# Second combination, normalisation and router products moved into the second attention's block of a two-layer transformer kernel

## The reference, cut to what matters

```python
xn = _layernorm(x)
x = x + _L0_attn_ref(xn, ...) + _L0_ffn_ref(xn, ...)
xn = _layernorm(x)
x = x + _L1_attn_ref(xn, slope_rate, Wqkv, Wg, norm_w, Wo) + _L1_ffn_ref(xn, router_w, ...)

# _L1_attn_ref: 16 heads of 128, linear attention with a decay per head
qkv = silu(x @ Wqkv.T)                 # q, k, v of every head
out = scan over blocks: (q * q_decay) @ kv + ((q @ k.T) * diag_decay) @ v
out = out * rsqrt(mean(out * out) + eps) * norm_w
return (sigmoid(x @ Wg.T) * out) @ Wo.T

# _L1_ffn_ref: one of 8 experts per token
router_logits = x @ router_w.T         # the best logit chooses the expert, its sigmoid scales the row
```

## Time and profile before

| what | value |
|---|---|
| median of 3 runs | 1422.84 us (1420.04 to 1425.09) |
| profiled execution, its own time | 1426.64 us |
| its span in the profile | 1424.8 us |
| PE busy (matmul) | 1279.2 us, 90% |
| DVE, ACT, POOL busy | 658.3, 526.1, 702.4 us |
| first transfer of combine1 issued at | 418.39 us |
| first product of attention1 at | 485.15 us |
| attention1's head loop | 492.6 us to about 1186 us |

### The profile page before, as it was taken

One profiled execution on the slowest core, in us unless ns is written; L12 is line 12 of the kernel. 1 busy time (PEld: TensorE's weight loads), 2 busy tenths in 40 slices (PEclk: granted clock), 3 DMA queues, 4 the chain that ended last, 5 costly groups with the idle time before them and its releaser, 6 DMA issues. The chain is left out here.

```text
span 1424.8 us, 20402 instructions
## 1 busy us (share of the span) xinstructions
PE 1279.2 (90%) x7238; PEld 1039.0 (73%) x7267; DVE 658.3 (46%) x1346; ACT 526.1 (37%) x1122; POOL 702.4 (49%) x556
## 2 busy tenths in 40 slices
PE   4488799999955388999999999999999996999999
PEld 4366588788845377888888888888888883666655
DVE  4698555565426247654554443534343341222223
ACT  2344466565535322333433334333343331111110
POOL 3343466676633646666776654756555540000014
PEclk9999999999985699999999999999999997999999
DMA  6700277777745321122212112111111106511113
GB/s 219 267 1 1 62 155 157 149 155 154 166 109 172 109 63 34 53 66 69 75 45 67 48 60 64 49 60 34 60 49 34 45 0 244 202 45 45 45 59 115
DMA packets 98483, 128.43 MB, mean 90 GB/s; under 512 B 11728, under 2 KB 81232, under 8 KB 98256
## 3 DMA queue, kind: packets, MB, share of 16 engines
q1 hardware_dynamic: 83408, 100.90, 22.2%
q0 software_dynamic: 14976, 26.23, 9.6%
HBM read 98.88 MB, written 28.21 MB: 89 GB/s over the span
## 5 line engine op out<-in xcount | busy, mean ns | idle before, releaser
L1553 PE MATMUL a_p_p<-a_xr,a_wr 128*128 128x512 f32 x1152 | 307.9, 403 | 2.4 <-DVE g_x L1957 2.4
L1553 PEld LDWEIGHTS a_p_p<-a_xr,a_wr 128*128 128x128 f32 x1152 | 207.7, 189 | 41.2 <-DVE g_x L1957 3.1
L1786 POOL TENSOR_TENSOR a_sqsum<-a_sqsum,a_sq 128x512 f32<-128x512 f32 x60 | 77.7, 1296 | 221.9 <-ACT a_sq L1710 221.9
L365 POOL DMA_INDIRECT acc<-l_ye,g_slot_token x64 | 102.1, 1595 | 67.1 <-ACT l_ye L695 57.7
L1565 PE MATMUL a_p_p<-a_wvr,a_xr 128*128 128x512 f32 x384 | 105.8, 413 | 24.1 <-POOL a_wvr L1755 24.1
L1751 POOL TENSOR_TENSOR a_wr<-a_w,a_wr 128x768 fp32r<-128x768 f32 x64 | 124.2, 1942 | 1.7 <-DVE a_wr L1812 1.7
L1844 DVE SCALAR_TENSOR_TENSOR a_gated<-a_th,a_p_o 128x512 f32<-128x512 f32 x64 | 44.0, 688 | 159.9 <-ACT a_sq L1710 159.9
L1788 POOL TENSOR_TENSOR a_gr<-a_gated,a_gr 128x512 fp32r<-128x512 f32 x64 | 97.6, 1525 | 23.7 <-DVE a_gr L1848 23.7
L1221 POOL DMA_DIRECT2D out<-e_ye x24 | 13.1, 546 | 193.5 <-DVE e_ye L1371 193.5
L1615 PE MATMUL a_p_w<-a_gr,l_wo_r 128*128 128x512 f32 x384 | 100.1, 396 | 2.3 <-POOL a_gr L1788 2.3
L1565 PEld LDWEIGHTS a_p_p<-a_wvr,a_xr 128*128 128x128 f32 x384 | 69.5, 194 | 36.4 <-issue 24.2
(11 more groups left out here) (248 smaller groups left out, 2761.8 us busy)
## 6 DMA issues: line engine op xcount, KB each, us to landing
a_w<-in_Wqkg SPq DMA_DIRECT2D x64, 384.0 KB, 3.2
l_up<-in_gate_up SPq DMA_DIRECT2D x64, 192.0 KB
a_wv<-in_Wv SPq DMA_DIRECT2D x16, 512.0 KB, 4.3
e_up<-in_gate_up SPq DMA_DIRECT2D x8, 1024.0 KB, 13.6
l_down<-in_down SPq DMA_DIRECT2D x64, 96.0 KB
acc<-l_zero SPq DMA_DIRECT2D x2, 2176.0 KB, 11.8
f_part<-acc SPq DMA_DIRECT2D x8, 512.0 KB, 6.2
e_down<-in_down SPq DMA_DIRECT2D x8, 512.0 KB, 12.3
```

Source lines behind the costliest of these rows:

```text
L365: pool.indirect_dma_start(g["acc"][e % 2][:, :], rows(e), ye[e % YR][:, :], None, compute_op=ALU.add)\
L1553: mm = pe.matmul(dst[:, :], wr[n % 2][:, wp, kk, c * P:(c + 1) * P], xr[n // H1 % 2][:, xp, kk, :], start=(kk, xp, wp) == (0, 0, 0), stop= ...
L1786: pool.tensor_tensor(sqsum[b % 2][:, :], sqsum[b % 2][:, :], sq[a % 2][:, :], ALU.add).then_inc(summed, 1)
```

## The change

`combine1` is gone, and its work stands in `attention1`, between the pieces of the prologue and in steps 0, 2, 5 and 8. The partial sums are loaded into tiles that the loop uses later (`qk` and `v[1]`), the raw output weights into `ywT`. The x of batches 0 and 1 is no longer read back from `cols1`, but split from `xT` as ACT leaves it there; `cols1` is still stored. A tile's logits share a PSUM bank with its transpose and are copied out tile by tile, where a copy of all stood at the end. The output weights are split in quarters: the first ahead of the loop, the others at n = 2, 5 and 8, by ACT in one operation for each head and by DVE (which takes the place of POOL). The pieces of the expert choice come later: `choose` at 2, the two rank products at the `state` of 3 and 4, `count` at 6, `place_experts` at 7, `place_rows` at 8, `tile_experts` at 9, `row` from 10 on.

```diff
-def combine1(nc, io, g):
...
+    CHOOSE, RANKS, ROWS = 2, (3, 4), 10
...
+        wo = ywT[:, :, :].rearrange("p k n -> p (k n)").rearrange("p (h n) -> p h n", h=QUAD)
+        part = [[qk[:, 2 * i:2 * i + 2, :].rearrange("p a n -> p (a n)").rearrange("p (t d) -> p t d", t=DB) for i in range(2)],
+                [v[1][:, 2 * i:2 * i + 2, :, :].rearrange("p t h e -> p (t h e)").rearrange("p (t d) -> p t d", t=DB) for i in range(2)]]
...
@@ sync @@
+            parts(0)
...
             values(0)
+            parts(1)
             weights(0)
+            output_weights(0)
             weights(1)
+            parts(2)
+            parts(3)
             values(1)
...
+            for c in range(DB):
+                store_columns(c)
             for n in range(LAST):
+                if n in (1, 4, 7):
+                    output_weights((n + 2) // 3)
                 if n + 2 < N:
                     weights(n + 2)
...
@@ tensor @@
+            def turn_x(t):
+                pe.wait_ge(xn_ready, t + 1)
+                if t >= 2:
+                    pe.wait_ge(logits_kept, t - 1)
+                for kk in range(KD):
+                    mm = pe.transpose(p_w[t % 2][:, kk * P:(kk + 1) * P], xn[t % 4][:, kk * P:(kk + 1) * P], g["ident"][:, :])
+                mm.then_inc(x_in_psum, 1)
+
+            def route_logits(t):
+                c, i = divmod(t, DB)
+                pe.wait_ge(xT_kept, t + 1)
+                for kk in range(KD):
+                    mm = pe.matmul(p_w[t % 2][:, 2 * P:2 * P + E1], xT[c % 2][:, kk, i * P:(i + 1) * P], router[:, kk, :],
+                                   start=kk == 0, stop=kk == KD - 1)
+                mm.then_inc(routed, 1)
+
+            def columns(c):
+                for t in range(DB * c, DB * (c + 1)):
+                    turn_x(t)
+                    if t % DB:
+                        route_logits(t - 1)
+                route_logits(DB * c + DB - 1)
...
-            for t in range(DB):
-                value(0, t)
+            pe.wait_ge(router_in, 16)
+            columns(0)
+            value(0, 0)
+            value(0, 1)
+            columns(1)
+            value(0, 2)
+            value(0, 3)
+            columns(2)
             for n in range(LAST):
                 a = n - 1
                 if n < N:
                     project(n, 0)
-                if n == 1:
-                    ranks()
                 if 0 <= a < N:
                     score(a)
                 if n < N:
                     project(n, 1)
+                if n == 0:
+                    columns(3)
...
@@ scalar @@
+            ins.then_inc(decays_done, 1)
+            root(0)
+            columns(0)
+            root(1)
+            high_output(0)
+            root(2)
+            value(0, 0)
+            value(0, 1)
+            columns(1)
+            root(3)
+            value(0, 2)
+            value(0, 3)
+            columns(2)
             for n in range(LAST):
...
+                if n == 0:
+                    columns(3)
+                if n in (2, 5, 8):
+                    high_output((n + 1) // 3)
...
@@ gpsimd @@
+            join(0)
+            low_v(0)
+            join(1)
+            low_w(0)
             low_x(0)
-            low_v(0)
-            low_w(0)
+            join(2)
+            pool.wait_ge(decays_done, 1)
+            pool.tensor_tensor(g["decay"][:, :, :], g["decay"][:, :, :], causal[:, :].unsqueeze(1).to_broadcast([P, H1, P]),
+                               ALU.mult).then_inc(causal_done, 1)
+            join(3)
             low_w(1)
+            low_x(1)
             low_v(1)
...
@@ vector @@
+            def low_output(i):
+                dve.wait_ge(wo_high, i + 1)
+                for h in range(QUAD):
+                    at = QUAD * i + h
+                    ins = dve.scalar_tensor_tensor(g["wo_r"][:, 1, at, :], wo[:, h, :], half_norm[:, at:at + 1], g["wo_r"][:, 0, at, :],
+                                                   ALU.mult, ALU.subtract)
+                ins.then_inc(wo_parts, 1)
...
+            combine(0)
+            high_v(0)
+            normalise(0)
+            combine(1)
+            high_w(0)
             high_x(0)
-            high_v(0)
-            high_w(0)
+            normalise(1)
+            combine(2)
             high_w(1)
+            normalise(2)
+            combine(3)
+            high_x(1)
+            normalise(3)
+            dve.wait_ge(half_ready, 1)
+            low_output(0)
             high_v(1)
             for n in range(LAST):
...
+                if n in (2, 5, 8):
+                    low_output((n + 1) // 3)
                 route(n)
...
-                spent = combine1(nc, io, g)
-                spent += attention1(nc, io, g)
+                spent = attention1(nc, io, g)
```

More of the change, by code:

```diff
@@ L1609, in output @@
                 if n == 0:
-                    pe.wait_ge(rank_kept, 2)
+                    pe.wait_ge(logits_kept, NT)
+                if h % QUAD == 0 and n < H1:
+                    pe.wait_ge(wo_parts, h // QUAD + 1)
                 if h == 0 and n:
@@ L1710, in square, with root, columns @@
                 act.activation(sq[n % 2][:, :], p_o[:, :], ACT.Square).then_inc(squared, 1)
-            for t in range(DB):
-                value(0, t)
+            def root(c):
+                act.wait_ge(var_ready, c + 1)
+                act.activation(std[:, DB * c:DB * (c + 1)], veps[:, DB * c:DB * (c + 1)], ACT.Sqrt).then_inc(std_ready, 1)
+            def columns(c):
+                if c >= 2:
+                    act.wait_ge(cols_stored[c % 2], 16)
+                    act.wait_ge(x_parts, c - 1)
+                for t in range(DB * c, DB * (c + 1)):
+                    i = t % DB
+                    act.wait_ge(x_in_psum, t + 1)
+                    act.activation(xT[c % 2][:, :, i * P:(i + 1) * P], p_w[t % 2][:, 0:2 * P].rearrange("p (k n) -> p k n", k=KD), ACT.Copy)\
+                        .then_inc(xT_kept, 1)
+                    if i:
+                        keep_logits(t - 1)
+                keep_logits(DB * c + DB - 1)
@@ new lines, in _ @@
+            act.wait_ge(c_in, 96)
+            act.activation(g["kdec"][:, :], slope[:, :], ACT.Exp, scale=back[:, :])
+            act.activation(g["bdec"][:, :], slope[:, :], ACT.Exp, scale=float(-P))
+            act.wait_ge(slope_ready, 1)
+            for h in range(H1):
+                act.activation(g["qdec"][:, h, :], ramp[:, :], ACT.Exp, scale=minus_slope[:, h:h + 1])
+            for h in range(H1):
+                ins = act.activation(g["decay"][:, h, :], lag[:, :], ACT.Exp, scale=minus_slope[:, h:h + 1])
@@ new lines, in normalise @@
+            def normalise(c):
+                at = slice(DB * c, DB * (c + 1))
+                dve.wait_ge(std_ready, c + 1)
+                dve.reciprocal(g["norm"][:, at, 1], std[:, at]).then_inc(rstd_ready, 1)
+                dve.wait_ge(rstd_ready, c + 1)
+                for t in range(DB * c, DB * (c + 1)):
+                    if t >= 4:
+                        dve.wait_ge(x_in_psum, t - 3)
+                    dve.tensor_scalar(xn[t % 4][:, :], g["x"][:, t, :], g["norm"][:, t, 0:1], g["norm"][:, t, 1:2],
+                                      ALU.subtract, ALU.mult).then_inc(xn_ready, 1)
```

320 lines of the change are left out of this document (118 added, 202 removed).

## The result

| what | before | after |
|---|---|---|
| median | 1422.78 us, 8 runs (1418.70 to 1425.09) | 1410.82 us, 8 runs (1408.61 to 1420.03) |
| profiled execution, its span | 1426.64, 1424.8 us | 1409.83, 1408.0 us |
| first transfer of the changed stretch | 418.39 | 413.11 |
| first product of step 2, counted from that transfer | 96.0 | 79.5 |
| first expert product, counted from that transfer | 777.0 | 764.4 |

The medians differ by 12.0 us. The ratio after to before is 0.9928 with the interval 0.9912 to 0.9944, which makes it 10.2 us faster, between 8.0 and 12.5. The forecast was 7.2 us faster (a median of 1415.6), so its sign and range were right and its size too small.

The account below looks back on a forecast made before the run. PE was taken as the bound, at 10.37 us a loop step. A gain of 8.0 us by step 2 and 0.8 lost in the loop made -7.2 us, so median 1422.84 becomes 1415.6; range 1404 to 1424.

Parts of the forecast that it names:

- Part 1: Prologue up to the first value product: it can start at 447.8, 37.4 us earlier than 485.15.
- The round of 1.8 us: Per-tile round of transpose, logits and their copy in the prologue's chunks: 1.8 us, bounds 1.2 and 2.3.
- The lock: DVE against POOL: with POOL work queued, DVE gets one SBUF operation through per POOL operation; normalise(1) then ends at 457.2.
- Rival B: DVE gets its four prologue normalisations in between POOL's operations; all behind is 7.1 earlier, 1408.5 us; chance 0.25.
- The table loads: Prologue switches from Sqrt to Silu on ACT: 1.28 us per load, next activation right behind, without the 1.38 drain.
- part 2: Prologue from first value to step 2: most of the 37.4 given back; step 2 at 506.4, 8.0 us gained.
- rows 2: Busy times per stretch before the change: PE at granted clock 0.50, 1.2 GHz, between 440 and 460 us.
- rival C: Clock stays at 2.4 GHz through columns(2) and (3): 4.1 us less, 1411.5 us; chance 0.10.
- The loop: Head loop: new DVE pieces stall steps by 7.9 us together, 0.8 more than the 7.06 removed.
- Rival D: DVE's backlog at steps 2, 5 and 8 stalls attend each time: 21.2 instead of 7.9, 1428.9 us; chance 0.15.
- Rival E: Prologue chunks wait for each other across ACT, DVE and POOL, eight microseconds more: 1423.6 us; chance 0.08.
- old stall: In attend of step 4 before the change: 4.72 us waiting for DVE's decay; removing it gives 7.06 us.

Follow-up runs that it names:

- mask_late: The kernel after with POOL's masking of the decays moved behind join(2), low_w(1), join(3) and low_x(1): 1409.51 us, ratio 0.9866 to the kernel before.
- columns_together: The kernel after with columns(2) directly behind columns(1), and value(0, 2) and value(0, 3) after both: 1416.24 us, one run, against 1422.62 for the kernel before.
- tiles_last: The kernel after with 13 small tiles declared behind the large ones: 1410.91 us, ratio 0.9918 to the kernel before.
- all_together: The kernel after with mask_late's POOL order, tiles_last's declarations and output-weight quarters at steps 1, 3 and 11: 1399.92 us, ratio 0.9827 to the kernel before.
- all_again: The kernel of all_together, unchanged, run once more for its trace: 1404.19 us, one run, against 1430.13 for the kernel before.
- second pair of profiles: Kernels before and after, unedited, profiled once more: before 1425.01 us (one run), after 1416.89 us, ratio 0.9924.
- ranks_only: The kernel before with only the two rank products moved, from ahead of score(0) to behind attend(0): 1421.53 us, ratio 0.9960.

## Why the forecast was right, and where it was not

**Part 1 held.** The first root was forecast at 437.1 and came at 437.4, the first value product at 447.8 and came at 447.8 (432.07 and 442.47 in after's own time). The round of 1.8 us was near at the low clock: a chunk took 6.35 us against 6.7.

**The lock held, with its times.** The sum of combine(2) was forecast at 457.2 and came at 457.0; mask_late shows the cause by taking two of POOL's operations away. Rival B, where DVE gets in between, fell. The Trainium skill (SBUF, State Buffer, Who interferes with whom) has the engine that issues first take the ports. In this trace a POOL operation that is queued follows the last one at once, and DVE gets one normalisation for each of them, four in 11.73 us. By the Trainium skill alone rival B would have been open, and the rows decided it.

**The table loads held.** The load at 455.29 follows the root (455.06 + 0.21) at once, and the Silu begins 1.29 us after the load began. The Trainium skill (ScalarE: Activation LUTs, What ACT_TABLE_LOAD costs) adds a drain of 1.38 us. This trace doesn't have it: at both switches to Silu, 455.29 and 465.61, the load begins within 0.02 us of the root's end and Silu within 0.01 us of the load's.

**The step that failed** is the end of part 2: "begins columns(2) at 474.1 and ends it at 481.0. project(0, 0) and (0, 1) 4.8, columns(3) 6.8, project(0, 2) and value(1, 0) 4.8, with the clock low each time as in rows 2 and 4". Set beside the forecast's times, after has:

| | forecast | after, shifted by 5.3 | gained over the forecast |
|---|---|---|---|
| columns(2) begins | 474.1 | 472.5 | 1.6 |
| columns(2) ends | 481.0 | 477.2 | 3.8 |
| columns(3) begins (0.15 inside the products) | 485.8 | 479.9 | 5.9 |
| columns(3) ends | 492.6 | 484.6 | 8.0 |
| step 1 begins | 497.4 | 488.9 | 8.5 |
| step 2 begins | 506.4 | 497.9 | 8.5 |

Some 6.4 us of the 8.5 came in the two chunks and the products between. About 5 of them are the clock: 1.65 in each chunk (6.35 against 4.70 us) and 1.8 in the products (4.8 against 3.0). Most of the rest is that the forecast's chunk of 6.7 to 6.9 us was too long even at the low clock. The forecast had the clock as rival C, with a chance of 0.10, and priced only the products, at 4.1 in all. What misled me were rows 2: there no 512-column product stands anywhere near, and here one stands just ahead of each of these chunks; columns_together and the other profiles show that this counts. It wasn't sure in any one execution: tiles_last lost part of it in columns(3), all_together in both chunks. The chunks themselves, which rival C left at the slow pace, gained more than the products: 2.2 and 2.1 against 1.8 and 0.5. Another 1.6 us came from columns(1) and the root behind it, 0.8 each.

**The loop held in its sum.** Forecast 7.9 us of stalls, measured 9.0 between steps 2 and 10. By the pieces: PE's step 3 1.8 (forecast 1.75, with the wait of 1.0 exactly), step 4 and 5 0.2 each (not forecast: the rank products' own time), step 6 1.5 (forecast 0.4), step 9 5.3 (forecast 5.6, of it 3.4 of waiting, which the trace has as 3.44). In step 6 it was not the decay that came late but the copy of the counts, which stands behind the quarter in DVE's list, and whose PSUM bank PE's `state` needs; the forecast had missed that reader. That scalar_tensor_tensor falls under the lock is shown by its 5.02 us against 1.67 alone. Rival D, with three full stalls of 7.06, fell: steps 3, 6 and 9 cost 1.8, 1.5 and 5.3. Rival E, with 8 us more ahead of step 2, fell too: step 2 came 8.5 us earlier than forecast. The slow clock behind a stall, which the forecast took from the old one of 4.72 us, comes behind much shorter waits too: the 1.5 us at attend(8) in all_again cost 3.9.

**Not forecast at all** is the 0.045 us more that each later step takes, 2.2 us from step 10 to step 63, which tiles_last shows to come from the places of the tiles.

**The sum.** 16.5 at step 2 instead of 8.0; 9.0 in the loop less the 7.06 of the old stall, so 1.9 to 2.3 given back; 2.2 for the longer steps. That leaves 12, and the two profiles have 777.0 less 764.4, or 12.6; the second pair of profiles has 10.7, the runs 10.2 (8.0 to 12.5). The unforeseen gain and the unforeseen loss made the forecast look nearer than its steps were: 8.5 too little on one side, some 1 and 2.2 too little on the other. That they partly cancel is luck.

## What to carry to other kernels

Where DVE and POOL both work in SBUF, count DVE's operations, not their columns, against POOL's queue at that moment. Of the kinds that were held here (casts, scalings, sums and products of SBUF tiles, scans) each POOL operation lets one through. So put POOL's long work that nobody waits for behind its short work that somebody does, and leave DVE's list short where POOL's is full. Before taking a slow clock from a stretch of small products, look at what stands just ahead of them in the new order. Taking one piece out of a crowded step helps only if no other piece stands ready to be caught in its place.

## What was not expected of the hardware

- Transposes and products of 8 columns ran at 2.4 GHz for a whole chunk (1.00, 4.70 us) in 13 of 18 chunks right behind 512-column products, and at 1.2 GHz (0.50, 6.35 us) in all ten first chunks, where none are ahead. The clock isn't the kernel's alone: the same instructions had 0.76 and 1.00 in two executions, and the same wait of 1.5 us cost 2.3 or 3.9 us, as the clock stayed up behind it or fell.
- A step of 10.36 us takes 10.41 when some 6.5 KB of small tiles are declared ahead of the large ones, with the same instructions. Which tile it is, and how far it must move, was not tried.
- A cast of 8 columns took 1.79 us and a scan of 8 columns 2.31 beside POOL's 2.27 and 2.39, where a small operation took 0.17 alone. A reduce wasn't held (0.28 beside POOL).
- One moved call of four small products, in ranks_only, is worth 0.4% of the whole kernel (0.9960), half of what the change brings.
